# A decoder layer on one core: prologue and DMA order, row-tiled self-attention scores, and moved maxima

## What is computed

```python
# L = LayerNorm over the last axis, no gain or bias
x = x + attn(L(x))    # 32 query heads, 8 key/value heads, head size 16, causal softmax, @ wo
x = x + xattn(L(x))   # C_q = L(x) @ Wq_d (64), C_kv = ctx @ Wkv_d (32)
                      # scores = (C_q @ W_qk per head) . C_kv / sqrt(32), 16 heads
                      # softmax over 1500 keys, then values C_kv @ Wv_u
x = x + ffn(L(x))     # @ kernel + bias + LoRA of the batch's expert (gate) + a shared LoRA
```

## Time and profile before

| | us |
|---|---|
| median of 3 runs | 679.2 (679.02 to 682.49) |
| the profiled execution | 681.57 |
| its span in the trace | 679.6 |
| TensorE busy | 591.6 (87%) |
| VectorE busy | 442.2 (65%) |
| GpSimd busy | 424.9 (63%) |
| ScalarE busy | 303.8 (45%) |

### The profile page before, as it was taken

One profiled execution on the slowest core, in us unless ns is written; L12 is line 12 of the kernel. 1 busy time (PEld: TensorE's weight loads), 2 busy tenths in 40 slices (PEclk: granted clock), 3 DMA queues, 4 the chain that ended last, 5 costly groups with the idle time before them and its releaser, 6 DMA issues.

```text
span 679.6 us, 12918 instructions
## 1 busy us (share of the span) xinstructions
PE 591.6 (87%) x3856; PEld 306.8 (45%) x3856; DVE 442.2 (65%) x717; ACT 303.8 (45%) x641; POOL 424.9 (63%) x394
## 2 busy tenths in 40 slices
PE   4863988699999999998999999999999899986965
PEld 4331644353544554464456354455446444433322
DVE  2711796378776887489658867588758966745451
ACT  1330144335644374346534564337444744563450
POOL 5002027558965886598776896488659877789300
PEclk9895889799999999999989999999999999997896
DMA  8567630353116510481018311661048101100000
GB/s 310 211 210 245 236 119 18 78 210 166 43 29 228 211 44 1 115 323 57 17 42 271 154 43 31 225 215 43 1 130 333 32 15 47 43 9 1 22 1 14
DMA packets 31410, 77.22 MB, mean 114 GB/s; under 512 B 11378, under 2 KB 25042, under 8 KB 28915
## 3 DMA queue, kind: packets, MB, share of 16 engines
q1 hardware_dynamic: 31186, 75.36, 33.1%
q10 hardware_dynamic: 160, 1.05, 0.4%
HBM read 58.66 MB, written 2.88 MB: 91 GB/s over the span
## 4 chain that ended last, share of the span: by engine, by line
PE 62%; DVE 12%; issue 7%; POOL 6%; ACT 5%; SPq 3%; DMA 3%; POOLq 0%; ACTq 0%; DVEq 0%
PE st_ps L649 11%; PE mx_ps L677 10%; PE pv_ps L664 9%; POOL acc L1096 5%; PE mi_ps L459 4%; PE mi_ps L466 4%; PE mi_ps L453 4%; PE mi_ps L512 4%; SPq L371 3%; PE mi_ps L631 2%; DVE mx_p L1020 2%; DVE sm L982 2%; PE mi_ps L537 2%; DMA b_eff<-acc 2%; PE mi_ps L635 2%
## 5 line engine op out<-in xcount | busy, mean ns | idle before, releaser
L1096 POOL TENSOR_TENSOR acc<-acc,p_ring 125x448 f32<-125x448 f32 x300 | 359.8, 1199 | 49.2 <-ACT p_ring L833 23.5
L1020 DVE TENSOR_REDUCE mx_p<-mx_ps 128x1 f32<-128x500 f32 x336 | 210.7, 669 | 101.7 <-PE mx_ps L677 100.6
L833 ACT ACTIVATE p_ring<-st_ps 125x448 f32<-125x448 f32 x384 | 189.7, 544 | 171.4 <-PE st_ps L649 164.4
L649 PE MATMUL st_ps<-q_st,c_st 98*125 98x448 f32 x384 | 155.3, 432 | 13.4 <-ACT p_ring L833 7.7
L677 PE MATMUL mx_ps<-c_st,q_st 96*128 96x500 f32 x336 | 139.4, 446 | 14.9 <-DMA q_st<-q_hl 11.2
L649 PEld LDWEIGHTS st_ps<-q_st,c_st 98*125 98x125 f32 x384 | 68.7, 191 | 117.1 <-ACT p_ring L833 88.2
L1104 POOL TENSOR_TENSOR rstd<-mv,eps_col 128x1 f32<-128x1 f32 x24 | 4.6, 192 | 153.2 <-DVE mv L894 153.2
L664 PE MATMUL pv_ps<-p_ring,c_nat 125*32 125x448 f32 x768 | 94.4, 564 | 1.0 <-ACT p_ring L833 0.9
L677 PEld LDWEIGHTS mx_ps<-c_st,q_st 96*128 96x128 f32 x336 | 63.2, 196 | 41.4 <-issue 20.6
L1096 POOL TENSOR_TENSOR acc<-p_ring 125x448 f32<-125x448 f32 x30 | 36.6, 1221 | 27.3 <-ACT p_ring L833 27.3
L466 PE MATMUL mi_ps<-ctx_sb,wkv_sb 128*32 128x375 f32 x512 | 48.1, 496 | 0.7 <-DVE p L943 0.7
(11 more groups left out here) (111 smaller groups left out, 671.0 us busy)
## 6 DMA issues: line engine op xcount, KB each, us to landing
ctx_sb<-in_ctx_t SPq DMA_DIRECT2D x16, 3000.0 KB, 11.1
c_st<-ct_hl SPq DMA_DIRECT2D x192, 46.9 KB, 2.0
q_st<-q_hl SPq DMA_DIRECT2D x96, 56.0 KB, 2.0
x_sb<-in_x SPq DMA_DIRECT2D x16, 112.0 KB
out_y<-x3n SPq DMA_DIRECT2D x16, 112.0 KB
wq_sb<-in_wq SPq DMA_DIRECT2D x2, 512.0 KB, 4.4
ctx_sb<-in_lora_a SPq DMA_DIRECT2D x1, 1024.0 KB, 6.8
ctx_sb<-in_lora_b SPq DMA_DIRECT2D x1, 1024.0 KB, 8.7
```

Source lines behind the costliest of these rows:

```text
L649: mm(st_ps[unit % STB][0:KC, 0:HALF], c_st[:, b % 4, t * KT + k * KC:t * KT + (k + 1) * KC], q_st[:, b // 2 % 2, b % 2, half * HALF:(half ...
L833: act.activation(p_ring[:, unit % PR, :], st_ps[unit % STB][0:KC, 0:HALF], ACT.Exp, scale=float(L) ** -0.5).then_inc(exp_done, 1)
L1020: ve.tensor_reduce(mx_p[:, p:p + 1], mx_ps[unit % MXB][:, 0:KP], AX.X, ALU.max).then_inc(red_done, 1)
L1096: po.tensor_tensor(dst, first, p_ring[:, unit % PR, :].rearrange("p (h s) -> p h s", s=S), ALU.add).then_inc(acc_done, 1)
```

## The change

In the prologue, x is padded on the host and loaded by one DMA, without a wait for a memset. wk is loaded ahead of wq; the first context batch ahead of the LoRA weights, which go to three other tiles (kern_sb, ox and x3n); the second context batch and x of pair 1 are loaded ahead of the cross weights. ScalarE runs one exponential on a spare column at its start; TensorE runs eight matmuls on ident before T1. GpSimd makes gkron and does the masks before the first power. The first latents use another bank. LoRA matmuls and copies are spread over later places. a_eff and b_eff are issued after the first q; the first q is spread by SyncE and ScalarE, six DMAs each. The waits for eff_out and for the feed-forward weights move into or behind body 0.

In the bodies, S0 to S3 become SA and SB: two heads r each, contracted over 64 rows in two row tiles, which write to the two mi_ps banks, 224 columns a matmul (khat and gmask halve). VectorE adds the mask with two instructions a step. The three pieces of group 3 move from among the scores into its steps, between WA, SA, WB and SB (WA and WB are waits of TensorE only); NM comes ahead of SB on VectorE. SN1 goes ahead of AS. In group 9 the one piece among the scores and the two behind T2 become one ahead of T2, one ahead of CQ, one ahead of H, and on VectorE YT comes ahead of them. spread_q issues its eight high DMAs at H and its four low ones after spread_m at the odd MT.

The diff, without context lines and smaller declarations:

```diff
@@ -57,10 +57,10 @@
-IDENT_MADE, MASKS_MADE, PADS_MADE, ALL_MADE = 2, 6, 10, 12
-PIECES_IN = [3, 2, 4, 3, 0, 0, 0, 3, 4, 1, 3, 0]
+IDENT_MADE, MASKS_MADE, PADS_MADE, CST_MADE, ALL_MADE = 2, 6, 10, 11, 12
+PIECES_IN = [3, 2, 4, 0, 0, 0, 0, 3, 4, 0, 3, 0]
@@ -83,19 +83,20 @@
-    [("M", 1), ("S0", "n"), ("S1", "n"), ("S2", "n"), ("S3", "n"), ("SM0", "n"), ("NM", "m"), ("SM1", "n")],
+    [("WA", "n"), ("M", 1), ("SA", "n"), ("M", 2), ("WB", "n"), ("M", 1), ("NM", "m"), ("SB", "n"), ("SM0", "n"),
+     ("SM1", "n")],
-    [("CT", "b"), ("AS", "b"), ("SN1", "n")],
+    [("CT", "b"), ("SN1", "n"), ("AS", "b")],
-    [("YT", "f"), ("T2", "n"), ("M", 2), ("CQ", "n"), ("H", "n"), ("N2", "f")],
+    [("YT", "f"), ("M", 1), ("T2", "n"), ("M", 1), ("CQ", "n"), ("M", 1), ("H", "n"), ("N2", "f")],
-        "S0": 1, "S1": 0, "S2": 1, "S3": 0, "V": 0, "P0": 1, "P1": 0, "P2": 1, "P3": 0, "O1": 0, "Y": 1,
+        "SA": (0, 1), "SB": (0, 1), "V": 0, "P0": 1, "P1": 0, "P2": 1, "P3": 0, "O1": 0, "Y": 1,
@@ -169,7 +170,7 @@
-        khat = sb("khat", [128, 2, G, S])
+        khat = sb("khat", [128, 2, G // 2, S])
@@ -216,7 +218,9 @@
-        for s in x_in + ctx_in:
+        for s in x_in:
+            rates[s.name] = 16
+        for s in ctx_in:
@@ -287,8 +292,15 @@
         def step_bank(name, n):
+            if n == 0 and name in ("Ah", "A"):
+                return mx_ps[MXB - 1]
+        def spread_first_q(dma, part, dst, t):
+            dma(q_st[dst:dst + L, 0, :, t * 4 * S:(t + 1) * 4 * S].bitcast(F32),
+                q_hl[t * L:(t + 1) * L, part, :, :].bitcast(F32)).then_inc(q_in[0], 16)
@@ -332,8 +344,7 @@
-                for h in range(2):
-                    dma(x_sb[h * SLOT:h * SLOT + S, n % 2, :], x[pair_index(n), h]).then_inc(x_in[n % 2], 16)
+                dma(x_sb[:, n % 2, :], x[pair_index(n)].rearrange("b s d -> (b s) d")).then_inc(x_in[n % 2], 16)
@@ -360,13 +371,13 @@
-            def spread_q(n):
-                for part, dst in ((0, 0), (0, L), (1, 2 * L)):
-                    if dst == 0:
-                        sp.wait_ge(qh_hi, due(qh_hi, n + 1))
-                    if part == 1:
-                        sp.wait_ge(qh_lo, due(qh_lo, n + 1))
+            def spread_q(n, part, rows):
+                if part == 0:
+                    sp.wait_ge(qh_hi, due(qh_hi, n + 1))
+                else:
+                    sp.wait_ge(qh_lo, due(qh_lo, n + 1))
+                for dst in rows:
@@ -385,19 +396,22 @@
-            sp.wait_ge(dve_c, due(dve_c, 1))
+            dma(wk_sb[:, :, :], wk.rearrange("(c p) n -> p c n", p=128)).then_inc(w_attn, 16)
-            dma(wk_sb[:, :, :], wk.rearrange("(c p) n -> p c n", p=128)).then_inc(w_attn, 16)
-            for k in range(2):
-                dma(lora_raw[k], (lora_a, lora_b)[k].rearrange("n (e f) r -> (n e) (f r)", e=8)).then_inc(raw_in, 16)
+            load_ctx(0)
-            load_ctx(0)
+            a_rows, b_rows = (w.rearrange("n (e f) r -> (n e) (f r)", e=8) for w in (lora_a, lora_b))
+            dma(lora_raw[0], a_rows).then_inc(raw_in, 16)
+            dma(lora_raw[1], b_rows[:, 0:1536]).then_inc(raw_in, 16)
+            dma(lora_raw[2], b_rows[:, 1536:2048]).then_inc(raw_in, 16)
+            load_ctx(1)
+            load_x(1)
@@ -407,21 +421,24 @@
-            sp.wait_ge(lora_ps, due(lora_ps, 8))
-            load_ctx(1)
+            sp.wait_ge(qh_hi, due(qh_hi, 1))
+            for t in range(4):
+                spread_first_q(dma, 0, 0, t)
+            for t in range(2):
+                spread_first_q(dma, 0, L, t)
+            sp.wait_ge(lora_ps, due(lora_ps, 4))
-            sp.wait_ge(eff_out, due(eff_out, 32))
-            spread_q(0)
             def body(i):
-                    load_x(i + 1)
+                    if i:
+                        load_x(i + 1)
@@ -431,12 +448,17 @@
                         elif name == "MT":
+                            if n % 2 and n + 1 < B:
+                                spread_q((n + 1) // 2, 1, (2 * L,))
                         elif name == "H":
-                            spread_q(n)
+                            spread_q(n, 0, (0, L))
                         elif name == "F2":
+                if i == 0:
+                    sp.wait_ge(eff_out, due(eff_out, 32))
@@ -473,6 +495,14 @@
+                if name == "WA":
+                    pe.wait_ge(q1_sb, due(q1_sb, n + 1))
+                    pe.wait_ge(k_sb, due(k_sb, 2 * n + 2))
+                if name == "WB":
+                    pe.wait_ge(s1_sb, due(s1_sb, 4 * n + 2))
@@ -499,18 +529,15 @@
                 elif name == "Q1":
-                elif name in ("S0", "S1", "S2", "S3"):
-                    r = int(name[1])
-                    if r == 0:
-                        pe.wait_ge(q1_sb, due(q1_sb, n + 1))
-                        pe.wait_ge(k_sb, due(k_sb, 2 * n + 2))
-                    if r >= 2:
-                        pe.wait_ge(s1_sb, due(s1_sb, 4 * n + r - 1))
-                    for b in range(2):
-                        last = mm(o[b * SLOT:(b + 1) * SLOT, 0:G * S], qt[:, r, b * SLOT:(b + 1) * SLOT],
-                                  khat[:, b, :, :].rearrange("p g k -> p (g k)"), start=True, stop=True)
+                elif name in ("SA", "SB"):
+                    for j in range(2):
+                        r = 2 * (name == "SB") + j
+                        for half in range(2):
+                            rows = slice(half * 64, (half + 1) * 64)
+                            for b in range(2):
+                                last = mm(mi_ps[half][b * SLOT:(b + 1) * SLOT, j * 4 * S:(j + 1) * 4 * S],
+                                          qt[rows, r, b * SLOT:(b + 1) * SLOT],
+                                          khat[rows, b, :, :].rearrange("p g k -> p (g k)"), start=True, stop=True)
@@ -565,7 +592,7 @@
-                        pe.wait_ge(s1_sb, due(s1_sb, 2 * n + 3))
+                        pe.wait_ge(s1_sb, due(s1_sb, 2 * n + 4))
@@ -579,7 +606,7 @@
-                        pe.wait_ge(s1_sb, due(s1_sb, 2 * n + 8))
+                        pe.wait_ge(s1_sb, due(s1_sb, 2 * n + 7))
@@ -679,42 +706,46 @@
             def lora_factors(since, until):
-                pe.wait_ge(raw_in, due(raw_in, 16 * 3))
-                pe.wait_ge(dve_c, due(dve_c, 4))
+                pe.wait_ge(gk_done, due(gk_done, 1))
+                    part, k = (q // 4, q % 4) if q < 7 else (2, 0)
-                       lora_raw[q // 4][:, q % 4 * 512:(q % 4 + 1) * 512], start=True, stop=True)\
+                       lora_raw[part][:, k * 512:(k + 1) * 512], start=True, stop=True)\
+            for _ in range(8):
+                mm(mx_ps[0][:, 0:128], ident[:, :], ident[:, :], start=True, stop=True)
-            for name in ("K", "Qh", "Q1", "S0", "S1", "S2", "S3"):
+            for name in ("K", "Qh", "Q1", "WA", "SA", "WB", "SB"):
+            pe.wait_ge(w_latent, due(w_latent, 16))
+            for name in ("Ah", "A"):
+                step(name, 0)
-            pe.wait_ge(w_latent, due(w_latent, 16))
-            for name in ("Ah", "A", "V", "CT"):
+            for name in ("V", "CT", "P0", "P1"):
-            lora_factors(0, 6)
-            for name in ("P0", "P1", "P2", "P3", "O1"):
+            lora_factors(0, 2)
+            for name in ("P2", "P3", "O1"):
-            lora_factors(6, 8)
+            lora_factors(2, 3)
+            lora_factors(3, 7)
+            lora_factors(7, 8)
-            pe.wait_ge(w_ffn, due(w_ffn, 16 * 3))
-            pe.wait_ge(y_out, due(y_out, 16))
-            pe.wait_ge(pool_c, due(pool_c, ALL_MADE))
+            pe.wait_ge(pool_c, due(pool_c, CST_MADE))
@@ -732,6 +763,9 @@
+                if i == 0:
+                    pe.wait_ge(w_ffn, due(w_ffn, 16 * 3))
+                    pe.wait_ge(y_out, due(y_out, 16))
@@ -822,6 +856,9 @@
             def exponentials(b, g):
+                if b == 0 and g == 0:
+                    act.wait_ge(eff_out, due(eff_out, 32))
@@ -841,27 +878,39 @@
-            act.wait_ge(dve_c, due(dve_c, 2))
+            act.wait_ge(dve_c, due(dve_c, 1))
+            act.activation(table[:, :], minus_half[:, :], ACT.Exp)
-            for name in ("T1", "Q1", "SE0", "SE1", "A", "V", "CT"):
+            for name in ("T1", "Q1", "SE0", "SE1", "A"):
-            lora_out(0, 6)
-            for name in ("P0", "P1", "P2", "P3", "O1"):
+            act.wait_ge(dve_c, due(dve_c, 2))
+            for name in ("V", "CT", "P0", "P1"):
-            lora_out(6, 8)
+            lora_out(0, 2)
+            for name in ("P2", "P3", "O1"):
+                step(name, 0)
+            lora_out(2, 7)
+            step("T2", 0)
+            lora_out(7, 8)
+            for name in ("CQ", "H"):
+                step(name, 0)
+            act.wait_ge(qh_hi, due(qh_hi, 1))
+            for t in range(2, 4):
+                spread_first_q(act.dma_start, 0, L, t)
+            act.wait_ge(qh_lo, due(qh_lo, 1))
+            for t in range(4):
+                spread_first_q(act.dma_start, 1, 2 * L, t)
```

(50 more changed lines are left out.)

12 lines of the change are left out of this document (6 added, 6 removed).

## The result

The changed kernel takes 685.27 us (median of 8 runs, 680.1 to 688.57), the kernel before 679.89 beside it (8 runs, 674.89 to 682.49): a ratio of 1.0082 with a 95% interval of 1.005 to 1.0114, so it is slower by 0.8%. The profiled execution took 688.57 us with a span of 686.5, against 681.57 and 679.6 before; it is the longest of its eight, 3.3 above their median, so sums read from its trace come out larger than the difference of the medians. TensorE is busy 592.9 us (591.6 before), VectorE 433.8 (442.2), GpSimd 428.3 (424.9): the engines have no more work. The table follows the first maxima of body 0 and the K product of each body through both traces.

The account below looks back on a forecast made before the run. TensorE was taken to set the bodies' pace, except in the scores stretch, bound by VectorE; the prologue was serial. Terms -13.9 + 4.8 + 0.3 + 5.1 = -3.7 us on the 679.2 median gave 675.5 us, range 661 to 684.

Parts of the forecast that it names:

- Prologue: From the kernel's start to body 0's first maxima: -8.7 up to q_hl's copy and -5.2 after it, -13.9 us (bounds -10, -16).
- The start: Prologue's beginning: no wait for VectorE, one x DMA, activation table loaded early; -2.3 us (bounds -1.6, -2.9).
- P0: Prologue: P0 goes ahead of the LoRA matmuls and starts at 26.7 instead of 35.50, -8.8 us.
- the two LoRA matmuls ahead of P2: Prologue: two records of 512 columns each, priced at 0.9 us a matmul, ending at 29.5.
- W1's end: Prologue: with one LoRA matmul in place of two before Wh, it goes from 45.3 to 37.0, -8.3 us.
- The spread: Prologue, first q: SP and ACT issue six DMAs each, 5.4 us instead of 10.6, so -5.2.
- Scores stage: Self-attention scores in the bodies: VectorE bounds them, P2 0.8 us later; +4.8 in bodies 1 to 6, +0.3 in body 0.
- rival 3: Scores in the bodies: row tiles don't overlap, SA 0.9 later in seven bodies, +6.3, 681.8 us; chance 0.10.
- Rival 1: Scores in the bodies: VectorE isn't the bound, each body gets back 1.4, -8.4 in place of +5.1, 662.0 us; chance 0.20.
- The 0.19 for leaving tiles: Scores in the bodies: cost in us of an exit from tiled matmuls, of which SA and SB make one more.
- End of the bodies: First maximum waits for q's low part: +0.75 us in bodies 1 to 6, +0.6 in body 0, +5.1 (bounds 0, +7.5).
- rival 2: Bodies: TensorE's new waits let its clock fall from 2.4 to 1.2 GHz; +9 in six bodies, 684.5 us; chance 0.12.

Follow-up runs that it names:

- q_first_old_scores: The changed kernel with all twelve DMAs of q issued at H and the old scores stage put back: 684.04 us, ratio 1.0056 to the kernel before.
- after_straight: The changed kernel with bodies 1 to 6 in one round of the loop in place of three: 675.72 us, ratio 0.9918 to the kernel before.
- q_first_straight: q_first with bodies 1 to 6 in one round of the loop in place of three: 668.24 us, ratio 0.9807 to the kernel before.
- q_first: The changed kernel with all twelve DMAs of q issued at H again, ahead of the maxima rows: 676.84 us, ratio 0.9922 to the kernel before.
- before_q_split: The kernel before with one edit, the four low DMAs of q issued behind the two of the maxima rows: 696.29 us, ratio 1.0193 to the kernel before.
- after_filled_wait: The changed kernel with eight unused matmuls on ident in TensorE's wait before the first maximum: 680.21 us, ratio 0.9994 to the kernel before.
- m_rows_by_act: q_first with the odd batches' rows of maxima issued by ScalarE: 674.98 us, ratio 0.9929 to the kernel before.
- q_first_sp_shifted: q_first with 24 satisfied waits in SP's program ahead of the bodies: 671.06 us, ratio 0.9844 to the kernel before.
- before_straight: The kernel before with bodies 1 to 6 in one round of the loop in place of three: 677.77 us, ratio 0.9946 to the kernel before.
- before_sp_shifted: The kernel before with 24 satisfied waits in SP's program ahead of the bodies: 680.59 us, ratio 1.0032 to the kernel before.
- q_first_pe_shifted: q_first_straight with 96 satisfied waits in TensorE's program ahead of the bodies: 672.25 us, ratio 0.9871 to the kernel before.
- rows_by_act_straight: m_rows_by_act with bodies 1 to 6 in one round of the loop in place of three: 668.47 us, ratio 0.9797 to the kernel before.

## Why the prediction was wrong

The forecast was 675.5 us (661 to 684), a gain of 3.7; measured were 685.3, a loss of 5.4 against the kernel before beside it. By its steps:

- **Prologue**, -13.9 forecast, -11.15 measured. The start gave 0.7 in place of 2.3: K went from 10.63 to 9.97 and still waited 2.33 us for wv. x came early enough (statistics at 3.56), but the DMA engines were busy 79% of the first 10 us, so earlier issue brought the four weights less. P0 gained 7.4 in place of 8.8; the two LoRA matmuls ahead of P2 took 2.66 us, not 1.8; W1's end gained 5.2 in place of 8.3, and q_hl's high copy 6.3 (54.06 to 47.74) in place of 8.7. The spread gained 4.8 of the 5.2 forecast. By the Trainium skill, DMA: Bandwidth & Descriptors, "Issuing engines are not separate DMA queues", issuing from several engines saves the initiating time. The trace agrees, both queues issue at once:

```profile
47.76 3.89 SPq L302 DMA_DIRECT2D q_st<-q_hl  x6
...
47.76 4.21 ACTq L302 DMA_DIRECT2D q_st<-q_hl  x6
...
53.51 0.76 PE L704 MATMUL mx_ps<-c_st,q_st 96*128 96x500 f32 x1 [6.39 <-DMA q_st<-q_hl]
```

- **Scores stage**, +0.8 a body forecast; from K to P0 the bodies of the changed kernel are 0.2 to 0.4 shorter. The order of VectorE came as I drew it, the prices were too high: the pair of additions took 1.16 us, not 1.38, and the copy of the negated maxima (L1083) took 0.17 where I had carried over the 0.90 of the earlier trace rows. That 0.90 isn't a price of the copy: in before it takes 0.17 to 0.90 us, in the changed kernel's bodies 1 to 6 0.17 to 0.24. What lengthens it wasn't tried. TensorE's rows as expected: 0.99 us for 16 records, so row tiles do overlap (rival 3 is out), and its saving stayed idle, as the 0.71 before the maximum behind WB and the waits for V and the exponentials show. Rival 1, which gave back 1.4 a body, is out as well. (The 0.19 for leaving tiles was a misreading: the 0.40 and 0.21 of the earlier trace rows are pieces of a chain. In the timeline the two score matmuls take 0.47 and 0.37.)
- **End of the bodies**, +0.75 a body forecast. This is the step that failed, by its size. The chain was right: rows of maxima, four issues, landing, first maximum. In straight code bodies 1 to 5 paid the 0.8 forecast for it (body 0 some 3, where I had 0.6). In the loop it cost 3 to 5 us, 19.6 in bodies 1 to 5 where the forecast was 3.75. First, SP's queue isn't even there. In bodies 1, 3 and 5 one of the eight issues of q was held by a q8 packet (1.36 to 1.73 us), so they ended at 195.32 in body 1, 0.4 behind the copy m_t for which the rows of maxima had to wait anyway. At the end of a round (body 2) two packets of q8 and four of q14 came in, the two issues of the maxima took 1.97, and the low part landed at 277.7, 3.2 us after its last issue began (3.9 in body 4), where I had put 2.0. Second, TensorE's wait rose to 1.4 to 3.0 us, and behind it the clock fell to 0.50, which cost 1.4 to 2.8 a body. I had that mechanism as rival 2 but set it in the scores stage, priced it at 9 us in all and put 0.12 on it. My upper bound for this step, 7.5 us, didn't hold either.
- **T2, CQ, H and the tail**, 0 forecast: H to F2 is 0.3 a body shorter, the last F2 comes 0.3 earlier after K of body 6.

What I should have seen in the trace of before: the end of the body had no slack. The rows of maxima were issued at 278.54 behind twelve issues, 1.7 us after their copy, and TensorE got them just in time. An edit that puts a further 2.6 us of issuing between that copy and an operand of TensorE has to be priced with the slowest issue and landing of the trace, and with a stretch at half clock behind it, rather than with the median of both. On the expectations: q_first_old_scores was missed by over 5 us (at most 679 expected, 684.0 measured), after_straight by 5 and q_first_straight by 4; q_first, before_q_split, after_filled_wait and m_rows_by_act moved the way expected but by less; q_first_sp_shifted moved more; before_straight, before_sp_shifted and q_first_pe_shifted were missed by their mechanism, the first because three of its sets became long in straight code. The others came near.

The best of these kernels are q_first_straight (668.2 us, 1.9% below before, interval 1.3 to 2.5%) and rows_by_act_straight (668.5, 2.0%, 1.7 to 2.4%): the change without the split of q, and without the rounds of the loop, the second with ScalarE's issue of the rows besides.

## What to carry to other kernels

In a queue that feeds the bounding engine, order is by the first reader: what a program reads first in its own order must be issued first, and an operand of a matmul that stands right behind in TensorE's order counts as much as the one that stands first. Waits of 1.4 to 3.0 us on a bounding TensorE cost here about twice their length, because the clock fell behind them, while waits of 1.1 us (before_q_split, bodies 1, 3 and 5) cost no more than themselves; price both cases, or fill the wait. And when parts of a change don't add, look at single issues and at the instruction queues before you doubt the parts: code that is moved changes where the loads fall. 24 waits that do nothing went with 5.8 us less of 677 in q_first, by intervals that just touch, and with no change in before.

## What the runs showed of the hardware

- One DMA issue of q on SP's queue takes 0.60 us (0.64 from start to start), and 0.9 to 2.1 us in 28 of the 36 sets of twelve in which an instruction load of q8 fell, and in none of 62 others. Of 165 issues of over 0.9 us in all traces, 162 end 0.2 to 0.45 us after such a load has landed.
- The end of a round of the loop cost up to 5 us in a body of 72 (m_rows_by_act), with TensorE standing twice without a wait that the profile names; six bodies in one round were 3 to 10 us faster over the whole kernel, with 7 fewer packets of q8 (39 and 32 in q_first). How much of this is the ends and how much the place of the code wasn't separated.
- Waits of 1.4 to 3.0 us on a TensorE that was busy before and after were followed by a stretch at a granted clock of 0.50 in all five bodies of the changed kernel; waits of 0.9 us (after_straight) and 1.1 us (before_q_split) in the same place by none. Waits of 1.5 us in the scores stage of q_first_old_scores were followed by it in bodies 3 and 5 and not in body 1.
- Two row tiles of 64 rows, with halves of 64 columns, ran 16 records of 224 columns in 0.99 us, where 16 records of 448 columns untiled in the rows took 3.42: half the columns in 0.29 of the time.
